# A fused cross-attention block on one core: first and last steps of the pipeline in another order

## The reference

```python
residual = query                                  # x: 4 x 1024 x 256, f32
Q = split(einsum('bsd,ed->bse', query, w_q) + b_q)     # 16 heads of 16
K = split(einsum('bsd,ed->bse', key, w_k) + b_k)       # key = value = ctx: 4 x 64 x 256
V = split(einsum('bsd,ed->bse', value, w_v) + b_v)
scores = einsum('bhqd,bhkd->bhqk', Q, K) / sqrt(16)
scores = where(mask[:, None] == 0, -1e9, scores)
ctx = merge(einsum('bhqk,bhkd->bhqd', softmax(scores), V))
out = einsum('bsd,ed->bse', ctx, w_o) + b_o + residual
mu, var = mean(out), mean((out - mu) ** 2)        # over the 256 columns
out = (out - mu) * rsqrt(var + 1e-5) * gamma + beta
```

## Time and profile before

| | us |
|---|---|
| median of 3 runs | 162.0 (160.46 to 162.09) |
| the profiled execution, its own time | 161.22 |
| its span, first to last instruction | 159.4 |
| PE busy | 135.6 |
| DVE busy | 124.9 |
| POOL busy | 112.9 |
| ACT busy | 94.6 |

### The profile page before, as it was taken

How to read it: one execution, slowest core, us unless ns; L and a number is a source line. 1 busy time by engine, 2 the same in 40 slices (tenths; PEclk the granted TensorE clock), 3 DMA queues, 4 the chain that set the end, 5 groups by cost and what they waited for, 6 DMA issues and landing times.

```text
span 159.4 us, 2934 instructions
## 1 busy us (share of the span) xinstructions
PE 135.6 (85%) x1008; PEld 85.1 (53%) x1008; DVE 124.9 (78%) x232; ACT 94.6 (59%) x166; POOL 112.9 (71%) x109
## 2 busy tenths in 40 slices
PE   0897967988999998999899989998999579999600
PEld 0665734655566656665566565656565335558400
DVE  0297663678779797979798979797989887999973
ACT  3379555976872757776777675837764825660320
POOL 5006432099998059999999999998981899668670
PEclk9999987999999999999999999999999999999965
DMA  4999957999689747209301930057003503001115
GB/s 155 337 295 295 301 131 160 303 254 317 126 203 303 156 136 217 48 13 247 141 0 24 244 132 0 2 122 274 3 2 69 198 0 132 0 4 73 59 68 197
DMA packets 10016, 22.88 MB, mean 143 GB/s; under 512 B 1553, under 2 KB 1809, under 8 KB 10001
## 3 DMA queue, kind: packets, MB, share of 16 engines
q1 hardware_dynamic: 9424, 21.76, 47.9%
q10 hardware_dynamic: 576, 0.92, 1.6%
HBM read 14.82 MB, written 4.19 MB: 119 GB/s over the span
## 4 chain that ended last, share of the span: by engine, by line
PE 49%; DVE 21%; POOL 15%; issue 6%; ACT 4%; DMA 3%; DVEq 0%; ACTq 0%; POOLq 0%
PE ps_w L445 12%; PE ps_w L366 9%; PE ps_s L394 7%; PE ps_w L337 7%; DVE nmax L673 6%; PE ps_s L421 5%; POOL y L905 4%; POOL y L902 4%; DMA wq_sb<-wq 3%; PE ps_s L400 3%; DVE turned L693 3%; ACT y L591 2%; PE ps_w L378 2%; DVE cn L706 2%; POOL rstd L886 2%
## 5 line engine op out<-in xcount | busy, mean ns | idle before, releaser
L673 DVE TENSOR_REDUCE nmax<-ps_w 128x8 f32<-128x512 f32 x56 | 37.7, 678 | 16.3 <-PE ps_w L366 15.8
L578 ACT ACTIVATE probs<-ps_s 128x512 f32<-128x512 f32 x64 | 33.0, 603 | 19.4 <-PE ps_s L405 19.4
L837 POOL TENSOR_TENSOR xt_l<-xt_sb,xt_h 128x1024 fp32r<-128x1024 f32 x7 | 16.6, 2373 | 28.3 <-ACT xt_h L539 13.1
L445 PE MATMUL ps_w<-wo_sb,cn 128*128 128x256 f32 x112 | 29.3, 387 | 3.9 <-DVE cn L706 3.6
L366 PEld LDWEIGHTS ps_w<-k_half,q_mask 128*128 128x128 f32 x112 | 17.2, 190 | 24.1 <-DVE nmax L673 18.4
L366 PE MATMUL ps_w<-k_half,q_mask 128*128 128x256 f32 x112 | 27.9, 335 | 1.6 <-DVE nmax L673 1.1
L445 PEld LDWEIGHTS ps_w<-wo_sb,cn 128*128 128x128 f32 x112 | 19.4, 189 | 9.2 <-DVE cn L706 5.5
L591 ACT ACTIVATE y<-res,shift,rstd 128x256 f32<-128x256 f32 x28 | 14.8, 591 | 12.3 <-POOL shift L888 12.2
L693 DVE STREAM_TRANSPOSE turned<-ps_s 128x1024 f32<-128x1024 f32 x16 | 19.8, 1239 | 0.8 <-PE ps_s L421 0.8
L902 POOL TENSOR_TENSOR y<-y,brow 128x512 f32<-128x512 f32 x13 | 16.6, 1279 | 4.4 <-ACT y L591 4.1
L394 PE MATMUL ps_s<-q_sb,k_pair 32*128 32x512 f32 x128 | 19.1, 668 | 0.0
(11 more groups left out here) (78 smaller groups left out, 201.5 us busy)
## 6 DMA issues: line engine op xcount, KB each, us to landing
m_sb<-maskT SPq DMA_DIRECT2D x32, 128.0 KB, 6.5
x_sb<-x SPq DMA_DIRECT2D x8, 512.0 KB, 4.5
xt_sb<-xT SPq DMA_DIRECT2D x7, 512.0 KB, 6.7
q_mask<-mask SPq DMA_DIRECT2D x28, 128.0 KB, 2.5
out<-y SPq DMA_DIRECT2D x6, 512.0 KB, 3.2
xt_sb<-xT SPq DMA_DIRECT2D x2, 256.0 KB, 5.4
out<-xt_sb SPq DMA_DIRECT2D x2, 256.0 KB, 2.0
brow<-bias_rows SPq DMA_DIRECT2D x1, 384.0 KB, 5.6
```

Source lines behind the costliest of these rows:

```text
L445: return pe.matmul(tile_outputs(c, i)[:, t], cn[:, c % 2, j, (2 * i + t) * P:(2 * i + t + 1) * P], wo_sb[:, j], start=j == 0 and c < LAST, ...
L578: act.activation(probs[:, g % 2, quad], ps_s[:, quad], ACT.Exp).then_inc(e_done, 1)
L673: dve.tensor_reduce(nmax[:, c % 2, t].rearrange("p (q r) -> p q r", r=32)[:, :, 2 * j:2 * j + 2], max_bank(c, i).rearrange("p (q h k) -> p ...
```

## The change

At the start:

- The key projection of chunk 0 is taken out in halves: DVE makes `kt` of group 0 and from it the two pieces of `k_half`, then the same for group 1. `max_scores(0, 0)` waits for two pieces, `max_scores(0, 4)` for four.
- The first query projection issues the four products of high parts first and then the others, group by group; ACT takes out group 0 of the first queries before the high part of chunk 1.
- The values of batch 3 are projected behind the first two maxima; the projections of chunk 1 stand later in PE's list: group 0 between maxima 4, 5 and 6, group 1 behind maximum 7.
- DVE converts mask 1 behind maximum 3, and masks 0 and 2 behind the last maximum of chunk 0. Since `mask_done` counts conversions, the waits are translated by `masks_done`. POOL makes `k_pair` only after the first conversion.

At the end, PE's step 6 is written out separately:

- The maxima of chunk 7 use both `ps_w` banks in turn; outputs (4, 1), (5, 0), (5, 1) and later are placed around them. The first part of the scores of group (7, 0) is issued ahead of the turned maxima.
- DVE's list of step 6 has `divide(5, 1)` and `residual(4, 1)` behind the second maximum, and maxima 3 to 7 without anything between them.
- POOL's list has `with_bias(6)`, `deviations(4)`, `with_bias(7)` ahead of `affine(4)`; both halves of `deviations` ahead of both halves of `affine` for chunk 5; and for chunk 6 both, and those of chunk 7 in one go over four tiles, ahead of `affine(6, 0)`.
- ACT copies gamma and beta ahead of `normalised(6)`; DVE does `gammas` and `betas` before both halves of `scaled`; the stores of chunk 6 are both issued from ACT.

```diff
         def max_bank(c, i):
+            if c == LAST:
+                return ps_w[:, LAST_BANKS[i]]
...
+        def masks_done(c):
+            return (2, 1)[c] if c < 2 else c + 1
...
             def copy_mask(c):
-                sp.wait_ge(mask_done, c + 1)
+                sp.wait_ge(mask_done, masks_done(c))
...
             def project_first_queries():
                 pe.wait_ge(wqh_done, 1)
+                for d, high in ((0, xh_first), (1, xh_done)):
+                    pe.wait_ge(high, 1)
+                    for j in range(2):
+                        pe.matmul(query_bank(0, j), wq_h[:, d, j * P:(j + 1) * P], xt_h[:, 0, d],
+                                  start=d == 0, stop=False)
                 pe.wait_ge(wql_done, 1)
...
-                    pe.wait_ge(khalf_done, 4 * (b + 1))
+                    pe.wait_ge(khalf_done, 2 if c == 0 else 4 * (b + 1))
...
+                elif c == LAST:
+                    if i == 0:
+                        pe.wait_ge(qe_done, GROUPS)
+                    elif i == 1:
+                        pe.wait_ge(neg_done, LAST)
+                    elif i == 3:
+                        pe.wait_ge(res_done, GROUPS - 6)
+                    else:
+                        pe.wait_ge(nm_done, HALVES * c + (i if i == 2 else i - 1))
...
-            project_values()
+            project_values(range(3))
             max_scores(0, 0)
             max_scores(0, 1)
+            project_values((3,))
             max_scores(0, 2)
-            for j in range(2):
-                for d in range(PC):
-                    project_queries(1, j, (d,))
-                    max_scores(0, 3 + 2 * j + d)
+            max_scores(0, 3)
+            max_scores(0, 4)
+            project_queries(1, 0, (0,))
+            max_scores(0, 5)
+            project_queries(1, 0, (1,))
+            max_scores(0, 6)
             max_scores(0, 7)
+            project_queries(1, 1)
             turn_max(0)
-            for s in range(CHUNKS):
+            for s in range(LAST - 1):
...
+            scores(LAST - 1, 0)
+            max_scores(LAST, 0)
+            max_scores(LAST, 1)
+            values(LAST - 2, 1)
+            max_scores(LAST, 2)
+            output(LAST - 3, 1, 0)
+            output(LAST - 3, 1, 1)
+            scores(LAST - 1, 1)
+            max_scores(LAST, 3)
+            max_scores(LAST, 4)
+            values(LAST - 1, 0)
+            max_scores(LAST, 5)
+            max_scores(LAST, 6)
+            max_scores(LAST, 7)
+            scores_and_mask(LAST, 0)
+            output(LAST - 2, 0, 0)
+            turn_max(LAST)
+            output(LAST - 2, 0, 1)
+            scores_less_max(LAST, 0)
+            values(LAST - 1, 1)
...
# ACT
             identity_rows(0)
+            first_queries_out(0)
             high_x(1)
-            first_queries_out(0)
             first_queries_out(1)
...
-            normalised(LAST - 1, (0, 1))
             act.wait_ge(div_done, GROUPS)
             act.activation(ps_s[:, 1]...brow[:, 2:4], ACT.Copy).then_inc(gb_done, 1)
+            normalised(LAST - 1, (0, 1))
             normalised(LAST - 1, (2, 3))
...
# DVE
             for j in range(2):
+                keys(j)
+                first_half_keys(j)
             for i in range(HALVES):
                 maxima(0, i)
-                if i in (4, 5):
-                    mask_values(i - 4)
+                if i == 3:
+                    mask_values(1)
+            mask_values(0)
             mask_values(2)
...
+            maxima(LAST, 0)
+            maxima(LAST, 1)
+            divide(LAST - 2, 1)
+            residual(LAST - 3, 1)
+            maxima(LAST, 2)
+            moments(LAST - 3, 1)
+            for i in range(3, HALVES):
+                maxima(LAST, i)
+            divide(LAST - 1, 0)
+            residual(LAST - 2, 0)
+            moments(LAST - 2, 0)
             divide(LAST - 1, 1)
...
+            gammas()
+            betas()
             scaled(0)
-            gammas()
             scaled(1)
-            betas()
...
# POOL
             low_x(1)
+            pool.wait_ge(mask_done, 1)
             pair_keys(0)
...
+            affine(LAST - 4, 0)
+            affine(LAST - 4, 1)
+            with_bias(LAST - 1)
+            deviations(LAST - 3)
+            with_bias(LAST)
             affine(LAST - 3, 0)
             affine(LAST - 3, 1)
-            with_bias(LAST)
             deviations(LAST - 2, slice(0, 2))
+            deviations(LAST - 2, slice(2, 4))
             affine(LAST - 2, 0)
-            deviations(LAST - 2, slice(2, 4))
             affine(LAST - 2, 1)
             deviations(LAST - 1, slice(0, 2))
+            deviations(LAST - 1, slice(2, 4))
+            last_deviations()
             affine(LAST - 1, 0)
-            deviations(LAST - 1, slice(2, 4))
-            last_deviations(0)
-            last_deviations(1)
```

More of the change, by code:

```diff
@@ L280, in _ @@
             store(LAST - 2)
-            for c, i in ((LAST - 1, 0), (LAST, 0), (LAST, 1)):
-                store_half(c, i)
+            for i in range(2):
+                store_last(i)
             for c in (LAST - 1, LAST):
@@ L295, in project_keys, with project_values @@
                 mm.then_inc(k_done, 1)
-            def project_values():
+            def project_values(batches):
                 pe.wait_ge(in_wv, 16)
-                for b in range(BATCHES):
+                for b in batches:
                     for d in range(PC):
@@ L310, in project_first_queries @@
                 pe.wait_ge(wqh_done, 1)
-                pe.wait_ge(wql_done, 1)
-                for d, high, low in ((0, xh_first, xl_first), (1, xh_done, xl_done)):
-                    pe.wait_ge(high, 1)
-                    pe.wait_ge(low, 1)
-                    for j in range(2):
[L316 to L321, removed]
+                for d, high in ((0, xh_first), (1, xh_done)):
[3 more added lines that the diff above has]
+                                  start=d == 0, stop=False)
+                pe.wait_ge(wql_done, 1)
+                for j in range(2):
+                    for d, low in ((0, xl_first), (1, xl_done)):
+                        pe.matmul(query_bank(0, j), wq_l[:, d, j * P:(j + 1) * P], xt_h[:, 0, d],
+                                  start=False, stop=False)
+                        if j == 0:
+                            pe.wait_ge(low, 1)
+                        mm = pe.matmul(query_bank(0, j), wq_h[:, d, j * P:(j + 1) * P], xt_l[:, 0, d],
+                                       start=False, stop=d == PC - 1)
+                    mm.then_inc(q_done, 1)
             def project_queries(c, j, part=range(PC)):
@@ L502, in _ @@
                 max_scores(front, 3)
-                if s >= 1 and ahead < CHUNKS:
+                if s >= 1:
                     project_queries(ahead, 0)
@@ L633, in _ @@
                 if s == LAST:
+                    normalised(LAST - 2, (0, 1))
                     normalised(LAST - 2, (2, 3))
@@ L654, in first_low_x, with keys, first_half_keys @@
                                       ALU.subtract).then_inc(done, 1)
-            def first_half_keys():
-                dve.wait_ge(kt_done, 2)
-                for j in range(2):
-                    for half in range(2):
-                        r = rows(half)
-                        dve.tensor_tensor(k_half[r, 0, half, j],
-                                          kt[r, j, 0].unsqueeze(1).to_broadcast([64, 4, KEYS]),
-                                          con[r, HALF_BLOCK:HALF_BLOCK + 4].unsqueeze(2).to_broadcast([64, 4, KEYS]),
-                                          ALU.mult).then_inc(khalf_done, 1)
+            def keys(j):
+                dve.tensor_scalar(kt[:, j], ps_w[:, 1, j * 256:j * 256 + 256].rearrange("p (b k) -> p b k", k=KEYS),
+                                  con[:, BIAS + 2 + j:BIAS + 3 + j], SCALE, ALU.add, ALU.mult).then_inc(kt_done, 1)
+            def first_half_keys(j):
+                dve.wait_ge(kt_done, j + 1)
+                for half in range(2):
+                    r = rows(half)
+                    dve.tensor_tensor(k_half[r, 0, half, j],
+                                      kt[r, j, 0].unsqueeze(1).to_broadcast([64, 4, KEYS]),
+                                      con[r, HALF_BLOCK:HALF_BLOCK + 4].unsqueeze(2).to_broadcast([64, 4, KEYS]),
+                                      ALU.mult).then_inc(khalf_done, 1)
             def maxima(c, i):
@@ L926, in _ @@
             pool.wait_ge(fill_done, 3)
-            for s in range(LAST):
+            for s in range(LAST - 1):
                 if s >= 3:
```

77 lines of the change are left out of this document (39 added, 38 removed).

## The result

The changed kernel takes 159.53 us (median of 20 runs, 157.39 to 161.19) against 161.89 us (20 runs, 160.43 to 164.22). The ratio is 0.9846, with a 95% interval of 0.9811 to 0.9882: 2.4 us or 1.5% faster. Forecast were 156.2 us and a range of 154.2 to 159.0. The sign was right, the time lies 0.5 us above the range, and the gain was less than half of the 5.0 us of the sum. The profiled execution has a span of 157.1 us against 159.4.

A forecast was written before the change was run, and what follows sets the result against it. No single bound was seen: PE carried 49% of the chain of waits, DVE 21%, POOL 15%. Start 2.25 plus end 2.75 gave 5.0 us off the profiled 161.22, so 156.2 us, range 154.2 to 159.0.

The forecast's parts named there:

- the landing of the mask copies: Start: the fourth copy of mask 1 lands at 23.4 us and PE starts chunk 1's maxima there, gaining 2.25 us.
- rival A: Start: the backlog does not hold the mask copies back, the start gains 3.3 us, 155.2 us in all; chance 0.2.
- The far bound of 24.5: Start: latest landing of the fourth mask copy, 5.6 us after an issue at 18.9; gain 1.15 us.
- The second step: Start: if the clock fell all the same, PE would be ready at 23.6, gain 2.0 us; the 2.25 hardly changes.
- The other steps of the start: Start: first maximum at 13.57, `turn_max` at 19.9, ACT free for `neg` at 21.43, moved mask conversions cost nothing.
- The end: Step 6 to the finish: 3.05 us saved in DVE's list less 0.3 for stores, a gain of 2.75 us.
- DVE's list: Step 6: 35.5 us of DVE work without idle time, ending at 153.85 instead of 156.89 us, 3.05 saved.
- POOL's late deviations: Step 6: moments (4, 1) end at 125.0 and POOL's deviations at 126.9; POOL's late start is absorbed.
- the load of x as the next wait: Step 6: chunk 7's load, issued at 123.4, lands 4.5 us later, so `with_bias(7)` starts at 127.95.
- The store term: End: four quarter-chunk stores issued close together cost between nothing and 0.7 us; 0.3 us lost was taken.
- Rival B: End: POOL gets `deviations(4)` 2.2 us later and sets the pace; the end gains 0.3, 158.7 us; chance 0.13.
- Rival C: Step 6: the granted clock falls and stays down, costing 8 us, 164.2 us in all; chance 0.05.

The follow-up runs named there:

- e6: The changed kernel with SP waiting for the mask 1 copies to land before issuing those of mask 2: 158.60 us, ratio 0.9842 to the kernel before.
- e3: The changed kernel with the loads of x for chunk 3 and bias rows issued behind the mask 1 copies: 155.55 us, ratio 0.9658 to the kernel before.
- e5: The changed kernel with the four copies of mask 1 issued by ACT instead of SP: 158.78 us, ratio 0.9835 to the kernel before.
- e4: The changed kernel with four spare matmuls on PE ahead of the maxima of chunk 1: 157.42 us, ratio 0.9770 to the kernel before.
- e7: From e3, both halves of `scaled` ahead of `gammas` and `betas`, chunk 6 stores reordered to match: 155.14 us, ratio 0.9623 to the kernel before.
- e8: From e3, POOL's old order: each half of `affine` of chunks 5 and 6 behind its half of `deviations`: 160.96 us, ratio 0.9967 to the kernel before.

## Why the prediction was wrong at the start and right at the end

**The step that failed** is the landing of the mask copies: "the backlog ends near 20.2 [...] so I put the fourth landing at 20.2 + 3.2 = 23.4". It was 24.73, 1.3 us later. The prediction had itself called this landing its weakest step. The stretches of the changed kernel show what the sum left out:

```profile
20.20:20.40 0.20, 0.20 (x4) 1.00 1.12 425
...
20.60:20.80 0.20, 0.20 (x4) 1.00 1.18 297
...
23.50:24.00 0.50, 0.00 (x0) 1.00 0.84 189
```

At 20.2 us the engines still move data at the speed of the loads (395 GB/s in the earlier trace rows); the lower speed of the mask copies begins near 20.6. From there it takes 3.4 us until the mean share falls at 24.0, about the 3.2 that I had taken. The rest, 0.7 us, is the tail in which few engines work (a share of 0.31 and less), and for that the sum had no term. I had taken the end of the backlog from the mean share of one half microsecond in the kernel before, where the last engines worked until 21.2. Started there, the same sum gives 24.4. How the 1.3 us divide among these parts is an estimate; e6 shows only that the copies of mask 2 are not most of it.

The reading that the copies wait for what is ahead of them was right (e3), and so was the choice against rival A. The rule of "DMA: Bandwidth & Descriptors" in the Trainium skill that I set beside it, the order within a ring, is not needed to explain the delay: issued from ACT, and so not behind the loads in SP's queue, the copies landed as late (e5). The far bound of 24.5, from the 5.6 us of the bias rows, was nearly exact, but in part by luck: that load is three times as large as a copy and was issued at 16.1 us, not behind the backlog but as the last part of it.

**The second step** is "if the clock fell all the same, PE would be ready at 23.6, gain 2.0; the 2.25 hardly depends on it". I had asked what the old fall of the clock, in the scores, was worth, and took it as gone once its idle time was gone. But the wait that I had put in its place left PE idle for 2.12 us, more than the 1.30 ahead of the old fall. The clock then fell at 26.5, 4 us after this idle time had begun, in the projection. I had the row for it, and did not ask what the new wait does to the clock.

How sure is it that the idle time brings the fall? For it: e4 fills the gap, and the fall is gone, worth 1.2 us. Of the twelve profiled executions, all seven with an idle time of PE of 1.3 us or more between 20 and 25 us show a fall before 30 us, and of the five without one only e7 does. Against it: e7 itself. So an idle time makes a fall likely, but it is not the only thing that does, and why it fell in e7 stays open. The Trainium skill's "TensorE: Matmul & The Clock Gate" was weighed in the prediction for the old gap only; the idle gaps that it says to avoid are longer than any of these, while here 1.3 us and 2.12 us had a fall behind them, and the stretch from 122.5 to 125.9, with 2.09 of 3.40 us busy, had none. From these runs no length of gap can be named that is safe.

Together: 2.25 forecast, -0.4 measured. When the maxima of chunk 1 start, the gain is 25.65 - 24.77 = 0.9, so the late landing took 1.4; by step 6 it is -0.4, so the half-rate clock took another 1.3. The other steps of the start held. `turn_max` came at 19.95 (19.9 forecast), the first maximum at 13.66 (13.57), `neg` behind ACT's list at 21.50 (21.43), and neither the conversions of masks 0 and 2 nor the moved low part stand in the chain that ended last.

**The end** was forecast step by step and came within 0.3 us. DVE's list 35.5 us, measured 35.2; moments (4, 1) and POOL's late deviations at +6.8 us behind the first maximum (6.6 forecast), the load of x as the next wait (9.4 behind, 9.6 forecast), POOL's idle behind moments (5, 1), and no wait of DVE for POOL. The store term was 0.3 forecast and 0.6 measured; it made up for the 0.3 by which DVE's list came out shorter, so that the total, 2.7 against 2.75, is nearer than its two terms. Rival B did not happen, but e8 shows how near it lies: POOL's order is what keeps it away. Rival C did not happen: the granted clock was 1.00 from 120 us to PE's last matmul.

None of the three rivals is what happened. B's time of 158.7 lies nearest to the 159.5, but by another path: it has the start gain and the end fail. C had the clock's fall, but at the end.

The range failed for the same reason as the forecast. Its upper end took a least gain of 1.15 us for the start, from the wait alone; the clock was not among the terms. With it the least gain of the start would have been near zero, which with the end's 2.0 and the spread of repeated runs gives 161.2 - 2.0 + 0.8 = 160.0 for the upper end, and 159.5 lies inside.

## What to carry to other kernels

When an edit removes one wait, price the one that takes its place twice: by its length, and by what the idle time does to TensorE's clock afterwards. Transfers that are wanted soon should be issued ahead of those wanted late: one line moved in SP's list was worth 3 us here, more than the whole change. A mean share of the DMA engines that falls does not mean that the last engine is free: a landing comes behind the tail, so add the tail, or look for the stretch in which the share is zero. And when an order of instructions is put back to see what it is worth, the lists of the other engines decide too: POOL's old order cost 5 us in e8, part of it because ACT's list had changed around it.

## What the runs showed of the hardware

- 128 KB copies within SBUF land 2.5 us after their issue on empty engines, and 4.7 to 5.6 us behind the loads of x, masks and bias rows, from SP's queue and, within 0.3 us, from ACT's (4.6 to 5.3).
- Four copies of 128 KB within SBUF moved at 184 to 215 GB/s with a share of the engines near one (22.0 to 22.6 us in the kernel before), where loads reached 395 GB/s.
- The tail of a loaded stretch lasted 0.6 us (kernel before, 20.6 to 21.2) and 1.2 us (e6, 22.4 to 23.6), with mean shares of 0.04 to 0.24, as much as one to four of 16 engines.
- The half-rate clock makes the same six projection matmuls take 2.90 instead of 1.39 us. It came behind idle times of PE of 1.3 and 2.1 us, and once (e7) with none over 0.55 us ahead of it; in every profiled execution the clock also falls behind PE's last matmul, where it costs nothing.
- Among the 20 runs of the changed kernel one had a mean granted clock of 0.984 and took 157.39 us; nine had 0.975 to 0.978 and 158.77 to 159.55, and ten 0.956 to 0.967 and 159.50 to 161.19. By 2 x (1 - clock) x span that is 5.0 us at 1.2 GHz for the first, some 7.2 for the nine and 10.4 to 13.9 for the ten. The profiled execution, one of the nine, shows where its half-rate time lies: about 3.4 us from 26.5 to 29.9, and 4.3 us behind PE's last matmul. By estimate the first run had only the second part, and no fall at the start. So the clock's falls differ from execution to execution of one kernel, and the one run that had least of them is 1.4 us shorter than any other, which agrees with e4. Where the half-rate time of the ten lies is open, since none of them was profiled.
